# Sixteen-head attention on one core: queries and attention products put into their rows by DMA, probability sums in sixteen rows a head

## The reference

```python
h = relu(x @ W1[lang] + b1[lang]);  u = x + h @ W2[lang] + b2[lang]       # adapter chosen per batch element
n = layernorm(u) * gamma[lang] + beta[lang]
q = (n @ Wq.T).reshape(b, t, 16, 16);  k = n @ Wk.T;  v = n @ Wv.T        # 16 query heads, one key and one value head
logits = einsum('btnh,bsh->bnts', q, k) / 4, causal mask (a window of 256 never cuts)
out = einsum('bnts,bsh->btnh', softmax(logits), v).reshape(b, t, 256)
x1 = x + out @ Wf.T + bf
y  = cond2(x1)   # 256 -> 1024 gelu -> 192 shared columns and 64 of a chosen expert
x2 = x1 + ffn(y) # gated 256 -> 1024, two 1024 x 1024 layers, 1024 -> 256, ternary weights
```

## Time and profile before

| | us |
|---|---|
| median of 3 runs | 1158.77 |
| lowest, highest | 1157.55, 1159.96 |
| the profiled execution, as timed | 1157.74 |
| its span in the trace | 1156.0 |

### The profile page before, as it was taken

One profiled execution on the slowest core, in us unless ns is written; L12 is line 12 of the kernel. 1 busy time (PEld: TensorE's weight loads), 2 busy tenths in 40 slices (PEclk: granted clock), 3 DMA queues, 4 the chain that ended last, 5 costly groups with the idle time before them and its releaser, 6 DMA issues.

```text
span 1156.0 us, 18793 instructions
## 1 busy us (share of the span) xinstructions
PE 1117.5 (97%) x6148; PEld 892.6 (77%) x6178; DVE 804.4 (70%) x1440; ACT 594.7 (51%) x989; POOL 214.6 (19%) x266
## 2 busy tenths in 40 slices
PE   4899999999998999999999999999999999999998
PEld 3567777777775788888888888888888888888886
DVE  2877777776776557756577875778656887568875
ACT  1355655555555634533365654556445565455653
POOL 2233333343345444452000000000000000000000
PEclk9999999999999999999999999999999999999999
DMA  4342122122143456654515443044440444304420
GB/s 122 111 149 60 53 59 63 48 60 63 47 160 124 151 187 202 227 188 150 204 35 164 140 167 115 10 164 146 162 137 0 163 146 163 137 8 145 145 91 37
DMA packets 66765, 135.97 MB, mean 118 GB/s; under 512 B 13793, under 2 KB 28017, under 8 KB 66545
## 3 DMA queue, kind: packets, MB, share of 16 engines
q1 hardware_dynamic: 57696, 114.49, 30.5%
q10 hardware_dynamic: 9024, 20.97, 5.0%
HBM read 107.65 MB, written 30.41 MB: 119 GB/s over the span
## 4 chain that ended last, share of the span: by engine, by line
PE 89%; DVE 6%; SPq 2%; issue 1%; DMA 1%; ACT 1%; POOL 0%; DVEq 0%; POOLq 0%; ACTq 0%
PE bank L1531 35%; PE bank L1493 10%; PE bank L1319 7%; PE bank L1543 5%; PE bank L1469 4%; PE bank L1463 4%; PE bank L1253 4%; PE bank L1234 3%; DVE neg_max L891 2%; PE bank L1274 2%; PE bank L1311 2%; PE bank L1216 2%; PE bank L1200 2%; PE bank L1237 1%; PE bank L1189 1%
## 5 line engine op out<-in xcount | busy, mean ns | idle before, releaser
L1531 PE MATMUL bank<-op_lo,w_ring 128*128 128x512 f32 x896 | 348.6, 389 | 0.0
L1531 PE MATMUL bank<-op_hi,w_ring 128*128 128x512 f32 x896 | 348.6, 389 | 0.0
L1066 DVE TENSOR_TENSOR op_lo<-x_blk,op_hi 128x512 fp32r<-128x512 f32 x288 | 193.8, 684 | 30.4 <-ACT op_hi L764 30.3
L764 ACT ACTIVATE op_hi<-x_blk 128x512 fp32r<-128x512 f32 x288 | 162.8, 620 | 73.6 <-PE bank L1531 69.3
L1531 PEld LDWEIGHTS bank<-op_lo,w_ring 128*128 128x128 f32 x896 | 168.2, 188 | 34.9
L1531 PEld LDWEIGHTS bank<-op_hi,w_ring 128*128 128x128 f32 x896 | 168.2, 188 | 34.9
L891 DVE TENSOR_REDUCE neg_max<-bank 128x2 f32<-128x512 f32 (+1 forms) x192 | 126.0, 685 | 48.0 <-remote 39.7
L617 ACT ACTIVATE p<-bank 128x512 f32<-128x512 f32 x192 | 111.3, 599 | 71.9 <-PE bank L1253 68.2
L788 ACT ACTIVATE x_blk<-x_blk,scales 128x512 f32<-128x512 f32 x96 | 69.3, 722 | 67.0 <-DVE x_blk L1119 28.9
L1493 PE MATMUL bank<-tile_hi,ffn_w 128*128 128x512 f32 x256 | 101.5, 396 | 0.0
L1493 PE MATMUL bank<-tile_lo,ffn_w 128*128 128x512 f32 x256 | 101.5, 396 | 0.0
(11 more groups left out here) (124 smaller groups left out, 1850.0 us busy)
## 6 DMA issues: line engine op xcount, KB each, us to landing
w_ring<-hid_scratch SPq DMA_DIRECT2D x112, 512.0 KB, 4.6
hid_scratch<-comb ACTq DMA_DIRECT2D x8, 1792.0 KB, 7.6
comb<-in_hid_d ACTq DMA_DIRECT2D x6, 768.0 KB, 5.1
xt<-in_x_t SPq DMA_DIRECT2D x16, 256.0 KB
xtok<-in_x_tok SPq DMA_DIRECT2D x16, 256.0 KB
resid<-in_x_t SPq DMA_DIRECT2D x16, 256.0 KB, 3.1
x_scratch<-x SPq DMA_DIRECT2D x16, 256.0 KB, 2.6
tile_in<-x_scratch SPq DMA_DIRECT2D x8, 512.0 KB, 4.1
```

What stands on the lines that cost most here:

```text
L764: nc.scalar.activation(op_hi[:, o % OP_RING, k], x_blk[:, operand_home(o), k], ACT.Copy).then_inc(s["op_hi"], 1)
L1066: nc.vector.tensor_tensor(op_lo[:, o % OP_RING, k], x_blk[:, operand_home(o), k], op_hi[:, o % OP_RING, k].bitcast(F32), ALU.subtract).the ...
L1531: last = mm(banks[first_bank + m][:, :], w, read(v[:, q % OP_RING, k, :]), start=k == 0 and v is op_hi and i not in (P2, P3), stop=k == KB ...
```

## The change

Queries, keys and values are now projected with features in the rows. The queries' two parts are put into the three row groups of each head of `q_t` by six DMAs on SP (`move_queries`), in place of 16 transposes on PE and four copies on ACT. The products of attention are put, 16 rows of values and 16 rows of sums for each head, into `att` and `sums` by eight DMAs on SP (`move_products`), in place of 12 transposes and one ACT copy. For that `values` has ones in all its sixteen upper columns, so that the sum of a head's probabilities stands in sixteen rows. The reciprocal is now taken of the tile `sums` (128 rows of 512) where it was taken of 128 rows of 16, twice. Key parts are made by ACT, values come through two transposes. Three slots of `q_t`, `keys` and `values` take the place of two, and the order in an iteration is new on every engine. Nothing changes in the second and third phase but the last element's tail, whose `project_out` and `add_residual` now stand behind the first tile of `cond2`.

```diff
+            def move_products(b):
+                sp.wait_ge(s["late_out"], b + 1)
+                sp.wait_ge(s["early_out"], b + 1)
+                settle(sp, "sp_settled")
+                for j in range(4):
+                    rows = slice(64 * (j % 2), 64 * (j % 2 + 1))
+                    sp.dma_start(att[rows, j // 2, :], pv[32 * j:32 * j + HD, :, :]).then_inc(s["pv_moved"], 16)
+                    sp.dma_start(sums[rows, j // 2, :], pv[32 * j + HD:32 * (j + 1), :, :]).then_inc(s["pv_moved"], 16)
+
+            def move_queries(n, slot):
+
+                sp.wait_ge(s["q_low"], n + 1)
+                settle(sp, "sp_settled")
+                for i, part in enumerate((q_high, q_rest, q_high)):
+                    for par in range(2):
+                        row = SLOT * par + HD * i
+                        sp.dma_start(q_t[slot][row:row + HD, :, :].bitcast(F32), part[:, par, :].bitcast(F32)).then_inc(s["q_moved"], 16)
...
-                    load_front(b + 3)
+                    l = load_inputs(b + 3)
+                    move_products(b - 1)
+                    load_rest(b + 3, l)
+                    move_queries(b + 2, (step + 2) % SLOTS)
                     store_x1(b - 1)
                     load_resid(b)
-                    move_maxima(b + 1, 1 - step % 2)
+                    move_maxima(b + 1, (step + 1) % SLOTS)
...
+            def queries_high(n):
+                act.wait_ge(s["q_mm"], n + 1)
+                if not is_first(n):
+                    act.wait_ge(s["q_moved"], 96 * n)
+                nc.scalar.activation(q_high[:, :, :], ring[0][:, :].rearrange("p (a t) -> p a t", a=2), ACT.Copy, scale=QSCALE).then_inc(s["q_hi"], 1)
+
+            def keys_high(n, slot):
+                act.wait_ge(s["kv_mm"], n + 1)
+                nc.scalar.activation(kv[:, :], ring[1][:, 0:T], ACT.Copy).then_inc(s["kv_out"], 1)
+                act.wait_ge(s["kv_out"], n + 1)
+                for par in range(2):
+                    nc.scalar.activation(keys[slot][:, par, :], kv[:, :], ACT.Identity,
+                                         bias=key_row[:, 2 * par:2 * par + 1], scale=key_row[:, 2 * par + 1:2 * par + 2]).then_inc(s["keys_hi"], 1)
...
-            def attention(b, t):
-
-                dve.wait_ge(s["pv_t_mm"], NT * b + t + 1)
-                o = side[t][:, :].rearrange("p (h c) -> p h c", h=NH)
-                nc.vector.reciprocal(recip[:, t, :], o[:, :, HD]).then_inc(s["recip_done"], 1)
...
+            def attention(b):
+                dve.wait_ge(s["pv_moved"], 128 * (b + 1))
+                nc.vector.reciprocal(sums[:, :, :], sums[:, :, :]).then_inc(s["recip_done"], 1)
+                dve.wait_ge(s["recip_done"], b + 1)
+                if not is_first(b):
+                    dve.wait_ge(s["proj_mm"], b)
+                nc.vector.tensor_tensor(att_t[:, :, :], att[:, :, :], sums[:, :, :], ALU.mult).then_inc(s["att_out"], 1)
```

More of the change, by code:

```diff
@@ L644, in iteration @@
                     products_out(b - 1, True)
+                if softmax and not maxima:
+                    act.wait_ge(s["maxima_moved"], 64 * B)
+                    store_chunk(0)
                 if softmax:
-                    for u in range(0, 4):
-                        exponential(b, u)
-                if maxima:
-                    queries_out(b + 1, 1 - odd, 1, 0)
-                    queries_out(b + 1, 1 - odd, 1, 1)
-                if softmax:
-                    for u in range(4, 8):
+                    for u in range(0, 6):
                         exponential(b, u)
@@ L941, in iteration @@
                     maximum(b + 1, 3)
-                if tail:
-                    attention(b - 1, 0)
-                if maxima:
                     maximum(b + 1, 4)
-                if tail:
-                    attention(b - 1, 1)
-                if maxima:
-                    maximum(b + 1, 5)
                 if front:
@@ L952, in iteration @@
                 if maxima:
-                    for u in range(6, 10):
+                    for u in range(5, 8):
                         maximum(b + 1, u)
                 if front:
-                    keys_of(b + 2)
+                    queries_low(b + 2)
+                if maxima:
+                    maximum(b + 1, 8)
+                if front:
+                    keys_low(b + 2, (slot + 2) % SLOTS)
+                if maxima:
+                    maximum(b + 1, 9)
+                if tail:
+                    attention(b - 1)
                 if maxima:
@@ L1219, in max_scores, with project_keys @@
-            def max_scores(n, odd, u):
+                if tail:
+                    pe.wait_ge(s["late_out"], n - 2)
+                elif not is_first(n):
+                    pe.wait_ge(s["q_low"], n)
+                for m in range(KD):
+                    for k in range(KD):
+                        last = mm(ring[0][:, m * T:(m + 1) * T], wq[:, k, m * P:(m + 1) * P], norm_t[:, k, :], start=k == 0, stop=k == KD - 1)
+                last.then_inc(s["q_mm"], 1)
+            def project_keys(n, tail):
+                if tail:
+                    pe.wait_ge(s["early_out"], n - 2)
+                elif not is_first(n):
+                    pe.wait_ge(s["keys_out"], 2 * n)
+                    pe.wait_ge(s["values_out"], 2 * n)
+                for k in range(KD):
+                    last = mm(ring[1][:, 0:T], wkv[:, k, :], norm_t[:, k, :], start=k == 0, stop=k == KD - 1)
+                last.then_inc(s["kv_mm"], 1)
@@ L1382, in iteration @@
                 if softmax:
[L1383 removed]
+                    scores(b, slot, 7)
+                if front:
+                    project_queries(b + 2, tail)
                 if maxima:
[L1385 removed]
+                    max_scores(b + 1, ahead, 8)
                 if softmax:
[L1387 removed]
+                    scores(b, slot, 8)
+                if front:
+                    project_keys(b + 2, tail)
                 if maxima:
[L1389 removed]
```

497 lines of the change are left out of this document (205 added, 292 removed).

## The result

The changed kernel takes **1308.01 us** (median of 4, 1305.62 to 1308.67) beside 1159.37 of the kernel before on the same chip: ratio **1.128 [1.126, 1.130]**. The forecast was 1253 with a range up to 1290. The sign and most steps of the path hold; the loss is 149 us where 94 was forecast. The profiled execution has a span of 1306.2 us, 150.2 longer than that of before.

What follows compares the result with a forecast made beforehand. PE bound the kernel; a chain of waits through all engines would stretch iterations from 21.56 to 27.9 us. 13 iterations give 82, start 5, end 7: 94 on 1157.74, so 1252, stated as 1253; range 1190 to 1290 (8 in 10).

Steps and rivals of the forecast that it cites:

- The reciprocal: On DVE in attention, 512 elements a row: 3.5 us, on the path of each iteration.
- S: Start of `adapter_in` on PE, from which an iteration's times are counted; the next one was forecast at S + 27.9 us.
- the products' moves hidden: Eight product DMAs on SP ahead of attention: landed by S + 17.5, hidden by 3.5 us.
- Rival 2: Reciprocal on DVE is short, 0.7 us: an iteration of 25.1, 1211 us in all; chance 0.12.
- 3: Rival: waits on DVE mostly don't come, an iteration of 22.3 us remains, 1179 in all; chance 0.10.
- 4: Rival: PE stays the bound and wins 2.8 us an iteration, so faster, 1121 us; chance 0.11.
- step 1: Normalising, from the root's end to PE's first projection: 2.67 us, reaching S + 14.6.
- step 2: Output projection on PE behind attention's reciprocal and multiplication: 1.77 us.
- rival 1: Granted clock falls in PE's waits, project_out on the path: 1.7 us in 13 iterations, 22, 1275 in all; chance 0.20.
- step 3: Start: first queries through six DMAs, and a longer way from normalising to queries in iteration -1: 5 us (2 to 9).
- The end: Iterations 14 and 15: product DMAs behind more loads and the expert ids, then the reciprocal: 7 us (0 to 12).
- PE loses: Work taken from PE by fewer transposes, net of additions: 2.9 to 3.4 us an iteration, 2.8 taken as won.

Runs made afterwards that it cites:

- written out: The changed kernel with SP's loop over the full iterations unrolled in the source, nothing else: 1288.3 us, ratio 1.113 to the kernel before.
- early root: The changed kernel with POOL's reciprocal root placed between the first and second mask instead of behind the second: 1281.1 us, ratio 1.106.
- filled waits: The changed kernel with unused matmuls of 0.21 us put into PE's four long waits: 1272.6 us, ratio 1.098.
- late filled: The changed kernel with attention at DVE's list end, its projection and residual an iteration later, PE order changed, root earlier, unused matmuls added: 1196.5 us, ratio 1.034.
- spread copies: The changed kernel with SP's large copies moved behind later iterations' moves and SP's loop unrolled: 1285.1 us, ratio 1.109.
- All together: late filled with SP's large copies spread and, at the end, the last products' moves ahead of expert ids and loads: 1196.3 us, ratio 1.033.
- copy for reciprocal: The changed kernel with a plain copy in place of the reciprocal of the sums: 1261.9 us, ratio 1.089.

## Why the prediction was wrong in size

**Right.** The reciprocal (3.35 for 3.5, on the path in full); first reduction at S + 5.3 (5.2); maxima landed S + 7.0 (6.8); root ended S + 11.5 (11.9); from the queries' projection to the end of `attention` 10.6 us (10.6); the products' moves hidden; PE idle ahead of project_out, released by DVE. Rival 2 (short reciprocal), 3 and 4 are out by the trace: 3.352 us, and PE busy 66 to 73%.

The estimate from the repeat count of 8 that the Trainium skill states for the reciprocal (VectorE: DVE Perf Modes, First, the fixed hardware budget) was 4.3 us; the trace has 3.352, and the measurement decides.

**Wrong, step 1: "Normalising until the first projection 2.67: S + 14.6".** It began at S + 16.2. The 2.67 became 4.69. The 0.73 of normalise became 1.56, since the third mask runs beside it; the forecast had moved `rstd_of` behind the second mask and counted its 0.64, but did not ask what POOL starts next. PE, which waited 2.41, then ran at half clock all the way to the projection, transposes and score units alike (3.07 us where it was 1.88 before, from 184.91 to 186.79), 1.2 more. The root, 0.4 sooner than forecast, gave 0.4 back. Removing the meeting gave 20 to 27 us (written out, early root). The transposes before:

```profile
184.91 0.66 PE L1183 MATMUL bank<-ident,norm 128*128 128x128 f32 x4
```

**Wrong, step 2: "project_out 1.77".** 3.42 at half clock, behind a wait of 3.2: next S 4.0 behind the attention's end in place of 2.7. This is rival 1, which had named this place and 22 us for it. Filling the waits gave 35 us alone, 2.7 an iteration. So rival 1's mechanism holds and was too small: the clock fell behind the wait for normalise too. Together 1.6 + 1.3 = 2.9 an iteration, the 30.8 less 27.9; some 2.5 of it is the clock. The forecast had left the clock out of its sum and given it a chance of 0.20.

**Wrong, step 3: the start, 5 us.** It is 20.6. The first queries came at 33.95 instead of 27.83, as the forecast had it in kind:

```profile
33.95 0.79 PE L1227 MATMUL bank<-keys,q_t 128*128 128x256 f32 x2 [5.57 <-DMA q_t<-q_high]
```

But this wait repeats for the next element, and PE is at a clock of 0.79 until 120 us. At the adapter's sum of iteration 1 the lag is 17.5 us (84.5 against 66.9). In filled waits, with a clock of 0.96 from 40 to 80 and nothing else changed, it is 15.3; in late filled, with 1.00, an earlier root and other edits, it is 11.8. So the clock alone is about 2 of it. About 12 stay even in late filled; I put them down to the queries' longer way in two iterations, which was not tried by itself. The large copies, behind which the moves of iteration 1 land, add 3 to 5 (spread copies against written out). I had not looked at what stands on SP there:

```profile
109.20 3.78 PE L1280 MATMUL bank<-att_t,wf 128*128 128x256 f32 x8 [9.44 <-DVE att_t L924]
```

**The end**, 7 forecast and 10.4 found by subtraction. The mechanism named is there: in iteration 15 the reciprocal waits 11.83 us for moves behind expert loads.

```profile
526.39 3.35 DVE L920 RECIPROCAL sums<-sums 128x512 f32<-128x512 f32 x1 [11.83 <-DMA sums<-pv]
```

Two slips in the prediction's sums change nothing: by its own terms PE loses 2.7 to 3.4 us (2.9 to 3.4 is written), and a reciprocal of 4.3 us gives 1263 (1262 is written).

Open: how the 12 us of the prologue divide among the added moves, and how much of the 10.4 at the end is that wait. All together shortened this wait and gained nothing; the next element's reciprocal waited instead.

## What to carry to other kernels

Work taken from the engine that bounds is worth nothing if its replacement makes it wait: here PE lost two to three us of work an iteration and got 8.8 us of waits (busy 22.06 of 30.83 us from 206.04 to 236.87). Every output projection behind a wait of 3.2 us or more in the full iterations took 3.4 to 3.8 us, at half clock for most or all of it; behind waits of 2.1 to 2.4 us the transposes ran at half clock in nine iterations and at the full one in two others. When a path is followed, ask at each step what else starts at that moment on the neighbour engine, and run the sum again with half the clock behind the long waits. A division belongs where the tile is small: 16 elements a row cost 0.25 us, 512 cost 3.35.

## What the runs showed of the hardware that I had not expected

- Reciprocal on DVE, float32: 3352 ns for 512 elements a row, 6.5 ns each, the same all 16 times. With the 253 ns for 16 elements of before that is an estimate of 6.25 ns for each element more and about 150 ns fixed.
- Normalise (two instructions of 256 elements) 0.73 us alone, 1.50 to 1.56 when POOL's mask starts with it, in iterations 2 to 12 of the changed kernel. The half that is held ends 0.14 to 0.15 us after the mask each time.
- The clock can be at half without a long wait right ahead: output projections of 3.1 to 3.6 us behind waits of 0.15 to 0.57 us (copy for reciprocal), where PE had been busy 0.62 of the 2.80 us before.
- A wait of SP in its loop costs tenths of a microsecond more than written out (first maximum move 2.47 to 2.76 us behind the residual, 2.26 written out; 2.44 to 2.70 and 2.28 in the kernel before, where it changed nothing, 1.0005).
- Unused matmuls of 0.21 us in the waits made kernels faster by 29 and 35 us; where a transfer was the bound, by nothing (1241.9 and 1240.8).
